# ScalarE writes the masks of units 33 to 46 into the score banks, in place of eight TensorE products per unit

## The chip, the cores and the metric

One core of one Trainium2 chip runs the whole program. The time is device microseconds (us) of one launch. Engines: PE is TensorE (PEld its weight loads, which overlap its matmuls), DVE is VectorE, ACT is ScalarE, POOL is GpSimd, SP is SyncE, which only issues transfers here.

## The reference

Three attention layers over 32 sequences of 64 tokens, 128 features, 16 heads of 64. Layer 0 is causal self-attention, layer 1 attends to a context and is followed by a feed-forward block, layer 2 attends to the same context with rotary embeddings. Each layer ends with a residual and a layer norm. The part that the change touches is layer 2:

```python
q = rope((x @ Wq).reshape(B, Sq, H, Dh)).transpose(0, 2, 1, 3) / sqrt(Dh)
k = rope((ctx @ Wk).reshape(B, Skv, H, Dh)).transpose(0, 2, 1, 3)
scores = jnp.einsum('bhqd,bhkd->bhqk', q, k)
scores = jnp.where(mask[:, None, None, :], scores, -1e9)
attn = jax.nn.softmax(scores, axis=-1)
out = jnp.einsum('bhqk,bhkd->bqhd', attn, v).reshape(B, Sq, H * Dh) @ Wo
```

## The kernel before

A unit is two sequences, 128 tokens, one to each half of the partitions. Each layer has 16 units, so there are 48: 0 to 15 are layer 0, 16 to 31 layer 1, 32 to 47 layer 2. The program runs in steps, -2 to 49, one for each unit with two ahead and two behind; every engine has its own list of work for a step, written by hand, and they meet through semaphores only. In step u the kernel computes the scores and the softmax of unit u, projects queries (u even) or keys (u odd) of units ahead, projects values of unit u, and finishes unit u-2 (weighted values, output product, layer norm).

**PSUM.** Four banks, `ps_a`, hold the scores of one unit. In layer 2 each holds 256 columns: four heads of 64 keys. Four other banks, `ps_p`, are a ring. `fills(u)` lists what PE puts into it in step u, in order, and who empties it: A for ACT, D for DVE. A fill waits until the bank of four fills before has been emptied. In a layer 2 step the list is PP0, PP1 (transposed probabilities of unit u-2, A), two projection banks (D), O0, O1 (weighted values of unit u-2, A), two projection banks (D), V0, V1 (values of unit u, A), Y (output product, D). A step whose follower projects queries (u odd, up to 43) adds T at its end, the transposed input that this projection reads; ACT copies it to `xT_hi` and DVE takes the rest, `xT_lo`. Steps 33 and 35 also hold a feed-forward chunk: FT, F1 (two banks, A, line 804) before Y, and F2 (line 734) after it.

**PE, step u of layer 2.** First `scores(u)`: wait until the exponentials of unit u-1 have been read out of the banks (`exped`), then eight small matmuls that put the mask of unit u into the four banks (line 561: a broadcast mask row times `fold`, two stacked 32x32 identities; `start=True`), then wait for the rotated keys, then 128 small matmuls that add the scores on top (line 571). PE uses 32x64 tiles of its array for both. Then the ring in the order above. PP1 (line 678) waits for `normed_rest`, the second half of the normalised probabilities, and the first projection bank after a T waits for `xT_hi` and `xT_lo`.

**DVE.** Row maxima (line 1029), two turned projection banks (line 956), two more, one half of the normalisation of unit u-1 (line 1074), sums of unit u (line 1059), reciprocal, then Y and its statistics, then `xT_lo` where there is a T (line 943). DVE runs in this order, so `xT_lo` stands ahead of the next unit's maxima.

**ACT.** The empties that `fills` gives it, and between them the exponentials, 8 instructions of 64 columns each half: PP0 and PP1 (line 793), exponentials 0 (line 827), O0 and O1 (line 781), exponentials 1, V0 and V1 (line 791), F1 if there is one, then `normalise_rest(u - 1)` (line 851, 8 instructions, which raise `normed_rest`), then T (line 784) if there is one.

**Masks in layers 0 and 1.** For units 1 to 30 (`masked_by_scalar`), ACT writes the mask into the banks ahead (`put_masks`, line 845), and PE's scores add onto it. Units 0, 31 and all of layer 2 have PE write it.

Of the kernel before, what the change touches and what calls it, by code (L numbers as in the profile page):

```python
# [7 lines left out]
ACT = mybir.ActivationFunctionType  # L8
# [5 lines left out]
B, S, E = 32, 64, 128  # L14
H, D = 16, 64
PAIRS = H // 2
UNITS = B // 2
# [3 lines left out]
N = LAYERS * UNITS  # L21
# [37 lines left out]
def split_heads(u):  # L59

    return 2 * UNITS <= u < N
# [32 lines left out]

def masked_by_scalar(u):

    return 0 < u < 2 * UNITS - 1


def turned_by(u):  # L100
# [180 lines left out]
def build(nc, a, out):  # L281
    ctx = ExitStack()
    with ctx:
# [250 lines left out]
        def _(pe):  # L534
# [7 lines left out]
            def scores(u):  # L542
# [6 lines left out]
                if layer == 2:  # L549
                    if u == 2 * UNITS:  # L550
                        pe.wait_ge(setup_dve, FOLD)

                        pe.wait_ge(headed, HEADED.before(u))


                    for i in range(4):
                        for b in range(2):
                            of = slice(32 * i, 32 * i + 32)
                            own = (i // 2) ^ b
                            m = mask[of, 1, u % UNITS, own:own + 1, :]  # L560
                            mm(ps_a[64 * b:64 * b + 64, i ^ b, 0:256], fold[of, :], m.broadcast_to([32, 4, S]),
                               start=True, stop=False, skip_group_check=True)

                    pe.wait_ge(rotated, ROTATED.at(u - 1 - v, "Kr", 3, v))
                    for quad in range(H // 4):
                        for half in range(2):
                            for i in range(4):
                                for b in range(2):
                                    t = (2 * v + b) * S
                                    of = slice(32 * i, 32 * i + 32)  # L570
                                    last = mm(ps_a[64 * b:64 * b + 64, i ^ b, 64 * quad:64 * quad + 64],  # L571
                                              qT[of, par, 2 * quad + half, t:t + S], kT[of, par, 2 * quad + half, t:t + S],
                                              start=False, stop=half == 1, skip_group_check=True)
                    last.then_inc(scored, 1)
                    return
# [175 lines left out]
            for u in range(FIRST, END):  # L751
                if u in (0, READY):
                    pe.wait_ge(setup_dve, MASKED if u else FIRST_MASKED)

                late = u % 2 == 0 and masked_by_scalar(u)
                if attends(u) and u != N - 1 and not late:
                    scores(u)
                if u - 1 in BIAS_STEPS:
# [17 lines left out]
        def _(act):  # L776
# [61 lines left out]

            def put_masks(u):

                act.wait_ge(setup_dve, FIRST_MASKED if u < READY else MASKED)
                m = mask[:, u // UNITS, u % UNITS, 0:1, :].broadcast_to([128, PAIRS, S])
                for j in range(2):
                    act.wait_ge(shifted, SHIFTED.at(u - 1, j))
                    nc.scalar.activation(ps_a[:, j, :].rearrange("q (p k) -> q p k", k=S), m, ACT.Copy).then_inc(masked, 1)  # L845
# [30 lines left out]
            for u in range(FIRST, END):  # L876
# [4 lines left out]
                if by_head(u):  # L881
# [4 lines left out]
                    for at, (name, j, who) in enumerate(fills(u)):  # L886
                        if "A" not in who:
                            continue
                        while waiting and ((name, j) == ("V", 0) or (name, j) == ("O", 0) and len(waiting) == 2):
                            exponentials(u, waiting.pop(0))  # L890
                        empty(u, at, name, j)
                        if (name, j) == (("F1", 1) if ffn_chunk(u) is not None else ("V", 1)):
                            split_high(u, after_input=True)
                            if by_head(u - 1):
                                normalise_rest(u - 1)
# [485 lines left out]
```

## Time and profile before

| | us |
|---|---|
| Median of 3 runs | 514.36 |
| Lowest and highest | 513.75 to 515.39 |
| The profiled execution, its own time | 513.52 |
| Span of that execution in the trace | 511.6 |
| PE busy | 495.3 (97%) |
| PE's weight loads busy | 462.6 (90%) |
| DVE busy | 426.8 (83%) |
| ACT busy | 394.2 (77%) |
| POOL busy | 315.0 (62%) |

The profiled execution took 1.9 us more than its span, and 0.84 us less than the median. Busy shares are averages over three layers; layer 2 runs from about 334 to 511 us of the span. A row of the timeline merges neighbouring instructions of one line: its length runs from the first start to the last end. Since an engine starts the next instruction before the recorded end of the one before, the time that an instruction really takes of its engine is read from start to start.

### The profile page before, as it was taken

The page shows a single profiled execution, that of the slowest core. Times are in us where ns is not written, and L with a number is a line of the kernel's source. Part 1 is how long each engine was busy: PE and PEld are TensorE (multiplying, and loading weights), DVE is VectorE, ACT ScalarE, POOL GpSimd, SP SyncE. Part 2 cuts the span into 40 slices and gives each one's busy share as a digit, 9 for nine tenths or more (in the row PEclk, how much of TensorE's full clock was granted, in tenths as well). Part 3 has the DMA queues.
Part 4 walks back from the last instruction along what each step waited for, and adds up shares of the span by engine and source line. Part 5 has one row for each costly group of instructions (what it writes and reads, how often), then busy time and mean ns, then how long its engine had stood idle before and what let it go on. Part 6 is the DMA issues. An engine that isn't in the chain of part 4 may idle for free.

```text
span 511.6 us, 23583 instructions
## 1 busy us (share of the span) xinstructions
PE 495.3 (97%) x10188; PEld 462.6 (90%) x10188; DVE 426.8 (83%) x757; ACT 394.2 (77%) x1048; POOL 315.0 (62%) x611
## 2 busy tenths in 40 slices
PE   8989999999999999999999999899999999999995
PEld 7879989989999999999999997789999999999985
DVE  5998988977899788777878779898989888889883
ACT  6877868868988788767878685778778887888761
POOL 3617567546448554454645338878777887788735
PEclk9999999999999999999999999999999999999999
DMA  8910000000021010000000000000000000000000
GB/s 244 361 64 14 3 13 13 9 8 13 3 83 46 5 42 3 2 4 2 3 3 3 3 3 3 2 4 3 4 6 10 15 8 9 8 14 8 9 8 24
DMA packets 10199, 13.79 MB, mean 27 GB/s; under 512 B 880, under 2 KB 7408, under 8 KB 10096
## 3 DMA queue, kind: packets, MB, share of 16 engines
q1 hardware_dynamic: 10096, 12.28, 7.6%
q8 instruction: 81, 1.33, 1.1%
q14 instruction: 22, 0.18, 0.1%
HBM read 11.23 MB, written 1.05 MB: 24 GB/s over the span
## 4 chain that ended last, share of the span: by engine, by line
PE 83%; DVE 6%; ACT 6%; POOL 3%; issue 2%; POOLq 0%; DVEq 0%; ACTq 0%
PE ps_p L712 15%; PE ps_p L538 9%; PE ps_p L539 8%; PE ps_p L540 8%; PE ps_p L678 7%; PE ps_a L597 6%; PE ps_a L619 6%; PE ps_a L571 4%; PE ps_p L667 4%; PE ps_p L669 4%; PE ps_p L668 4%; PE ps_p L619 3%; PE ps_p L734 2%; DVE turn L956 2%; ACT ps_a L845 1%
## 5 line engine op out<-in xcount | busy, mean ns | idle before, releaser
L712 PE MATMUL ps_p<-wo,headsT 128*128 128x128 f32 x768 | 94.0, 275 | 1.4 <-DVE headsT L964 0.9
L712 PEld LDWEIGHTS ps_p<-wo,headsT 128*128 128x128 f32 x768 | 90.4, 192 | 3.0 <-ACT headsT L781 1.0
L1248 POOL TENSOR_TENSOR small<-mv,epsilon 128x1 f32<-128x1 f32 x48 | 10.5, 218 | 133.2 <-DVE mv L985 133.2
L956 DVE TENSOR_TENSOR turn<-ps_p,rope 128x1024 f32<-128x1024 f32 x64 | 76.1, 1222 | 10.9 <-PE ps_p L540 9.3
L791 ACT ACTIVATE vv<-ps_p 128x512 f32<-128x512 f32 x96 | 56.2, 617 | 14.0 <-PE ps_p L669 12.2
L811 ACT ACTIVATE headsT<-ps_a 128x512 f32<-128x512 f32 x60 | 32.6, 596 | 39.5 <-PE ps_a L619 39.5
L827 ACT ACTIVATE probs<-ps_a,top 128x64 f32<-128x64 f32 x256 | 56.0, 354 | 5.8 <-DVE top L1029 3.1
L538 PE MATMUL ps_p<-xT_hi,wq_hi 128*128 128x256 f32 x192 | 59.0, 307 | 0.5 <-DVE xT_lo L943 0.3
L1059 DVE TENSOR_REDUCE total<-probs 128x16 f32<-128x1024 f32 x48 | 58.1, 1211 | 0.4 <-ACT probs L837 0.2
L1033 DVE TENSOR_REDUCE top<-ps_a 128x8 f32<-128x512 f32 x64 | 41.1, 684 | 20.7 <-PE ps_a L597 20.7
L799 ACT ACTIVATE qT<-ps_p,columns 128x256 f32<-128x256 f32 x126 | 49.0, 477 | 8.1 <-PE ps_p L540 8.1
L539 PE MATMUL ps_p<-xT_lo,wq_hi 128*128 128x256 f32 x192 | 54.5, 284 | 0.0
L540 PE MATMUL ps_p<-xT_hi,wq_lo 128*128 128x256 f32 x192 | 54.4, 283 | 0.0
L678 PE MATMUL ps_p<-eye,probs 128*128 128x128 f32 x384 | 51.1, 275 | 1.5 <-ACT vv L791 0.8
L678 PEld LDWEIGHTS ps_p<-eye,probs 128*128 128x128 f32 x384 | 43.4, 141 | 7.6 <-ACT vv L791 0.9
L1208 POOL TENSOR_TENSOR qT<-turn 128x512 f32<-128x512 f32 x32 | 43.6, 1386 | 8.4 <-DVE turn L956 8.4
L1208 POOL TENSOR_TENSOR kT<-turn 128x512 f32<-128x512 f32 (+1 forms) x40 | 44.9, 1148 | 5.2 <-DVE turn L956 5.2
L799 ACT ACTIVATE kT<-ps_p,columns 128x256 f32<-128x256 f32 x124 | 47.1, 497 | 0.7 <-PE ps_p L540 0.6
L1074 DVE TENSOR_TENSOR probs<-probs,rinv 128x512 f32<-128x512 f32 x62 | 44.2, 751 | 1.0
L962 DVE COPY probsT<-ps_p 128x512 f32<-128x512 f32 x58 | 37.2, 683 | 3.3 <-PE ps_p L678 3.3
L538 PE MATMUL ps_p<-cT_hi,wk_hi 128*128 128x256 f32 x128 | 39.0, 304 | 0.6
L538 PEld LDWEIGHTS ps_p<-xT_hi,wq_hi 128*128 128x128 f32 x192 | 37.3, 194 | 1.4 <-issue 0.4
(149 smaller groups left out, 1400.0 us busy)
## 6 DMA issues: line engine op xcount, KB each, us to landing
out<-y_out SPq DMA_DIRECT2D x16, 64.0 KB, 2.6
raw<-in_x_turned SPq DMA_DIRECT2D x1, 768.0 KB, 9.2
across<-in_across SPq DMA_DIRECT2D x1, 704.0 KB, 7.3
raw<-in_ctx_turned SPq DMA_DIRECT2D x5, 128.0 KB, 2.6
wq_raw<-in_L_xattn_sa_wq SPq DMA_DIRECT2D x2, 256.0 KB, 2.9
wk_raw<-in_L_xattn_sa_wk SPq DMA_DIRECT2D x2, 256.0 KB, 4.2
wv_raw<-in_L_xattn_sa_wv SPq DMA_DIRECT2D x1, 512.0 KB, 5.6
wo<-in_L_xattn_sa_wo SPq DMA_DIRECT2D x1, 512.0 KB, 6.7
```

The costliest lines, as they stand in the source:

```text
L538: mm(dst, w[0], x[0], start=True, stop=False)
L539: mm(dst, w[0], x[1], start=False, stop=False)
L540: return mm(dst, w[1], x[0], start=False, stop=True)
L619: before, last = last, mm(head_bank(u, b)[64 * c:64 * c + 64, 64 * p:64 * p + 64], vv[of, w % 2, c, p, :], probsT[of, p // HALF, q:q + 64] ...
L678: last = nc.tensor.transpose(bank[:, 128 * pp:128 * pp + 128], probs[:, unit % 2, at_head:at_head + 2, :].rearrange("q h k -> q (h k)"), e ...
L712: last = mm(bank[:, 0:E], headsT[:, p, :, :].rearrange("r b q -> r (b q)"), wo[:, layer % 2, p, :], start=(p == 0), stop=(p == PAIRS - 1))
L791: ins = nc.scalar.activation(vv[:, u % 2, j, :, :].rearrange("k p d -> k (p d)"), bank[:, :], ACT.Copy)
L799: ins = nc.scalar.activation(to[:, g % 2, p, :], bank[:, CT * k:CT * k + CT], ACT.Identity, bias=bias[:, g * CU // UNITS, p:p + 1])
L827: ins = nc.scalar.activation(probs[:, u % 2, n, :], ps_a[:, bank, 64 * k:64 * k + 64], ACT.Exp, bias=top[:, at:at + 1], scale=scale)
L956: ins = V.tensor_tensor(turn[:, j % 2, :, :].rearrange("d a (h b t) -> d a h b t", h=2, t=S), bank[:, None, :].broadcast_to([128, 2, 512]) ...
L1059: V.tensor_reduce(total[:, :], probs[:, u % 2, :, :], AX_X, ALU.add).then_inc(dve_step, 1)
L1208: G.tensor_tensor(to[:, projected(u) % 2, 2 * j:2 * j + 2, of], *[t[:, :, of] for t in turned(j)], ALU.add).then_inc(rotated, 1)
```

## The change

The masks of units 33 to 46 are written by ACT too. `put_masks(u)` gets a form for layer 2: it waits for the second half of the exponentials of unit u-1, which ACT itself has just issued, and writes the mask with two instructions, each over two banks of 256 columns. It stands directly behind the exponentials of the unit ahead, so ahead of V0 and V1. PE's eight mask matmuls of those 14 units go, and `scores` waits for `masked` in their place. Units 32 and 47 keep the matmuls. The condition `late`, which in layers 0 and 1 puts the scores of even units behind the weighted values, is held to those layers, so the place of the scores in layer 2 stays.

```diff
@@ def masked_by_scalar(u):
-    return 0 < u < 2 * UNITS - 1
+    return 0 < u < 2 * UNITS - 1 or 2 * UNITS < u < N - 1
@@ scores(u), layer == 2
-                    for i in range(4):
-                        for b in range(2):
-                            of = slice(32 * i, 32 * i + 32)
-                            own = (i // 2) ^ b
-                            m = mask[of, 1, u % UNITS, own:own + 1, :]
-                            mm(ps_a[64 * b:64 * b + 64, i ^ b, 0:256], fold[of, :], m.broadcast_to([32, 4, S]),
-                               start=True, stop=False, skip_group_check=True)
+                    if masked_by_scalar(u):
+                        pe.wait_ge(masked, MASKED_BANK.at(u - 1, 1))
+                    else:
+                        for i in range(4):
+                            for b in range(2):
+                                of = slice(32 * i, 32 * i + 32)
+                                own = (i // 2) ^ b
+                                m = mask[of, 1, u % UNITS, own:own + 1, :]
+                                mm(ps_a[64 * b:64 * b + 64, i ^ b, 0:256], fold[of, :], m.broadcast_to([32, 4, S]),
+                                   start=True, stop=False, skip_group_check=True)
@@ PE's loop over the steps
-                late = u % 2 == 0 and masked_by_scalar(u)
+                late = u % 2 == 0 and masked_by_scalar(u) and u < 2 * UNITS
@@ put_masks(u)
+                if split_heads(u):
+                    act.wait_ge(exped, EXPED.at(u - 1, 1))
+                    m = mask[:, 1, u % UNITS, 0:1, :]
+                    for j in range(2):
+                        nc.scalar.activation(ps_a[:, 2 * j:2 * j + 2, 0:256].rearrange("q m (f k) -> q m f k", k=S),
+                                             m[:, None, :, :].broadcast_to([128, 2, 4, S]), ACT.Copy).then_inc(masked, 1)
+                    return
@@ ACT's loop over fills(u), by_head(u)
                         while waiting and ((name, j) == ("V", 0) or (name, j) == ("O", 0) and len(waiting) == 2):
                             exponentials(u, waiting.pop(0))
+                            if not waiting and masked_by_scalar(u + 1):
+                                put_masks(u + 1)
```

ACT's order in step 37, a step of layer 2 that ends with a T, and into the next. Before (`ps_a` is read by the exponentials):

```order
L781 ACTIVATE headsT<-ps_p 128x8x64 [waits filled] x2
L827 ACTIVATE probs<-ps_a,top 128x64 [waits dve_step]
L827 ACTIVATE probs<-ps_a,top 128x64 x7
L791 ACTIVATE vv<-ps_p 128x512 [waits filled] x2
L851 ACTIVATE probs<-probs,inv 128x64 [waits dve_step]
L851 ACTIVATE probs<-probs,inv 128x64 x7
L784 ACTIVATE xT_hi<-ps_p 128x2x128 [waits filled]
```

After, the same place (the changed file's line numbers are 3 to 10 higher: 784 for 781, 830 for 827, 794 for 791, 861 for 851, 787 for 784):

```order
L784 ACTIVATE headsT<-ps_p 128x8x64 [waits filled] x2
L830 ACTIVATE probs<-ps_a,top 128x64 [waits dve_step]
L830 ACTIVATE probs<-ps_a,top 128x64 x7
L848 ACTIVATE ps_a<-mask 128x2x256 [waits exped]
L848 ACTIVATE ps_a<-mask 128x2x256
L794 ACTIVATE vv<-ps_p 128x512 [waits filled] x2
L861 ACTIVATE probs<-probs,inv 128x64 [waits dve_step]
L861 ACTIVATE probs<-probs,inv 128x64 x7
L787 ACTIVATE xT_hi<-ps_p 128x2x128 [waits filled]
```

Two instructions have come in, the first with a wait for ACT's own exponentials; V0 and V1, the normalisation and T all stand behind them. On PE, where step 38 ends and step 39 begins, before:

```order
L712 MATMUL ps_p<-wo,headsT 128x128 [waits act_emptied,dve_emptied]
L712 MATMUL ps_p<-wo,headsT 128x128 x7
L561 MATMUL ps_a<-mask,fold 64x256 [waits exped]
L561 MATMUL ps_a<-mask,fold 64x256 x7
L571 MATMUL ps_a<-kT,qT 64x64 [waits rotated]
L571 MATMUL ps_a<-kT,qT 64x64 x63
L678 MATMUL ps_p<-eye,probs 128x128 [waits normed,dve_emptied]
```

After (715 for 712, 574 for 571, 681 for 678):

```order
L715 MATMUL ps_p<-wo,headsT 128x128 [waits act_emptied,dve_emptied]
L715 MATMUL ps_p<-wo,headsT 128x128 x7
L574 MATMUL ps_a<-kT,qT 64x64 [waits rotated,masked,exped]
L574 MATMUL ps_a<-kT,qT 64x64 x63
L681 MATMUL ps_p<-eye,probs 128x128 [waits normed,dve_emptied]
```

The eight mask matmuls are gone, and their wait has moved to the first score matmul, with `masked` beside it. DVE, POOL and SP have the same rows in the same order as before.

## Rows read from the trace of the kernel before

**Rows 1.** The page: busy time of each engine, PE's granted clock in 40 slices.

```profile
PE 495.3 (97%) x10188; PEld 462.6 (90%) x10188; DVE 426.8 (83%) x757; ACT 394.2 (77%) x1048; POOL 315.0 (62%) x611
...
PEclk9999999999999999999999999999999999999999
```

**Rows 2.** Waits of PE's weight loads, 334 to 492 us: total us, times, longest.

```profile
PEld ps_a L561 <- issue: 1.3, 8, 0.2
PEld ps_p L678 <- ACT vv L791: 0.9, 1, 0.9
PEld ps_p L538 <- DVE turn L956: 0.6, 2, 0.3
```

**Rows 3.** Timeline of PEld and PE, step 38: start us, length us, engine, line.

```profile
402.26 0.12 PEld L561 LDWEIGHTS ps_a<-mask,fold 32*64 32x64 bf16 x8 [0.17 <-issue]
402.26 0.32 PE L561 MATMUL ps_a<-mask,fold 32*64 32x256 bf16 x8
402.29 1.51 PEld L571 LDWEIGHTS ps_a<-kT,qT 32*64 32x64 f32 x128
402.39 1.54 PE L571 MATMUL ps_a<-kT,qT 32*64 32x64 f32 x128
...
404.69 0.20 PEld L538 LDWEIGHTS ps_p<-xT_hi,wq_hi 128*128 128x128 f32 x1
```

**Rows 4.** Timeline of ACT, step 37 into step 38.

```profile
398.26 1.75 ACT L827 ACTIVATE probs<-ps_a,top 128x64 f32<-128x64 f32 x8
399.84 1.15 ACT L791 ACTIVATE vv<-ps_p 128x512 f32<-128x512 f32 x2
400.86 2.02 ACT L851 ACTIVATE probs<-probs,inv 128x64 f32<-128x64 f32 x8
402.77 0.38 ACT L784 ACTIVATE xT_hi<-ps_p 128x256 fp32r<-128x256 f32 x1
404.56 1.09 ACT L793 ACTIVATE probsT<-ps_p 128x512 f32<-128x512 f32 x2 [1.41 <-PE ps_p L678]
405.53 1.76 ACT L827 ACTIVATE probs<-ps_a,top 128x64 f32<-128x64 f32 x8
407.54 1.09 ACT L781 ACTIVATE headsT<-ps_p 128x512 f32<-128x512 f32 x2 [0.26 <-PE ps_p L619]
```

**Rows 5.** Timeline of ACT, steps 38 and 39, and PEld's transposes of step 39.

```profile
410.09 1.15 ACT L791 ACTIVATE vv<-ps_p 128x512 f32<-128x512 f32 x2
411.11 2.01 ACT L851 ACTIVATE probs<-probs,inv 128x64 f32<-128x64 f32 x8
...
420.13 1.15 ACT L791 ACTIVATE vv<-ps_p 128x512 f32<-128x512 f32 x2
...
413.90 0.86 PEld L678 LDWEIGHTS ps_p<-eye,probs 128*128 128x128 f32 x8
```

**Rows 6.** Timeline of ACT in layer 1: a pair of masks, and what follows.

```profile
201.25 1.11 ACT L845 ACTIVATE ps_a<-mask 128x512 f32<-128x512 bf16 x2
202.29 2.29 ACT L799 ACTIVATE qT<-ps_p,columns 128x256 f32<-128x256 f32 x6
```

**Rows 7.** Timeline of DVE, step 37 into step 38.

```profile
403.43 0.39 DVE L943 TENSOR_TENSOR xT_lo<-ps_p,xT_hi 128x256 fp32r<-128x256 f32 x1
403.97 1.22 DVE L1029 TENSOR_REDUCE top<-ps_a 128x16 f32<-128x1024 f32 x1 [0.15 <-PE ps_a L571]
405.79 2.36 DVE L956 TENSOR_TENSOR turn<-ps_p,rope 128x1024 f32<-128x1024 f32 x2 [0.59 <-PE ps_p L540]
```

**Rows 8.** Timeline of ACT and DVE across a T of the feed-forward step 35.

```profile
382.07 0.38 ACT L784 ACTIVATE xT_hi<-ps_p 128x256 fp32r<-128x256 f32 x1 [1.03 <-PE ps_p L657]
...
382.49 0.43 DVE L943 TENSOR_TENSOR xT_lo<-ps_p,xT_hi 128x256 fp32r<-128x256 f32 x1 [0.21 <-ACT xT_hi L784]
```

**Rows 9.** Timeline of ACT and PEld, feed-forward step 33.

```profile
350.59 1.76 ACT L827 ACTIVATE probs<-ps_a,top 128x64 f32<-128x64 f32 x8
352.17 1.22 ACT L791 ACTIVATE vv<-ps_p 128x512 f32<-128x512 f32 x2
353.49 1.57 ACT L804 ACTIVATE hT<-ps_p,columns 128x256 f32<-128x256 f32 x4
...
355.67 1.87 PEld L734 LDWEIGHTS ps_p<-w,hT 128*128 128x128 f32 x16
```

**Rows 10.** Timeline of ACT and PEld, feed-forward step 35.

```profile
374.51 1.76 ACT L827 ACTIVATE probs<-ps_a,top 128x64 f32<-128x64 f32 x8
...
379.76 1.87 PEld L734 LDWEIGHTS ps_p<-w,hT 128*128 128x128 f32 x16
```

## The prediction

> **What bounds the kernel now.** I read the page first: PE is busy 97% of the span, ACT 77%, and PE's granted clock stands in the top tenth in all 40 slices [rows 1], so PE runs at its upper level (2.4 GHz) throughout. Then the waits of PE in layer 2: between 334 and 492 us PE's loads waited for another engine some 1.5 us in all [rows 2]. So layer 2 is bound by PE's own list of work: steps take 10.25 and 10.04 us in turn, as the starts of V0 show (399.84, 410.09, 420.13), 20.29 for two [rows 4, 5].
>
> A bound PE does not mean that the others have room. The question is how much later ACT may finish before PE has to wait for it, so I read ACT's timeline over one step. ACT waits twice: 1.41 us ahead of PP and 0.26 us ahead of O [rows 4]. Everything between V0 and the next PP stands behind the new instructions, and two things of it are waited for by PE. One is `normed_rest` (the end of line 851), the other is `xT_hi` (line 784), through DVE's `xT_lo`.
>
> **What the change takes from PE.** In step 38 the loads of the mask matmuls start at 402.26 and those of the scores at 402.29; the matmuls start at 402.26 and 402.39 [rows 3]. Eight of them cost PE 0.03 us by the loads and 0.13 us by the matmuls, since they run side by side on different tiles. I take 0.13, as the matmuls' starts set when the scores end. 14 units: 1.8 us, at least 0.4. The gap of 0.17 ahead of them [rows 3] stays: the score matmuls use the same tiles.
>
> The Trainium skill, "TensorE: Matmul & The Clock Gate", Back-to-back issue gap, gives 262 cycles for an isolated matmul of 256 columns, 0.109 us. Eight in a row would be 0.87 us, and the change would take 12.2 us off PE, not 1.8. The trace has all eight behind each other's starts in 0.13 us, so it is the packing that the same page describes, and the row decides.
>
> **What it adds to ACT.** The nearest rows are the pairs of masks in layers 0 and 1: the same 512 columns from the same tile into PSUM. One pair starts at 201.25 and the next work at 202.29: 1.04 us [rows 6]. A wait comes with it. ACT starts V0 at 399.84, 0.17 us ahead of the recorded end of the exponentials (398.26 + 1.75 = 400.01) [rows 4]. The first mask waits for that end, and a releaser's end stands 0.04 us ahead of the waiter's start where I can see one (382.07 + 0.38 = 382.45, DVE at 382.49) [rows 8]. So ACT loses 0.17 + 0.04 = 0.21, and V0, V1, the normalisation and T come 1.04 + 0.21 = 1.25 us later. Call this A. From below: no overlap lost, A = 1.04. From above: the form over two banks has no row, and its two instructions might overlap nothing. One mask alone lasts 1.11 less half of 1.04, 0.59; two are 1.18, and with 0.21 A is about 1.40. I take 1.25, nearest to the rows of masks.
>
> The scores themselves do not wait for the masks. Both are written by 400.05 + 1.1 = 401.2, and PE comes to the scores at 402.26. V0's bank is wanted by a fill of the next step's PP, V0 drained at about 401.7: hidden too. If A passed 2.2 us both covers would be gone.
>
> **Where A meets PE: `normed_rest`.** In step 38 line 851 ends at 411.11 + 2.01 = 413.12. PE's loads for PP0 and PP1 start at 413.90, eight in 0.86, so the fifth, which needs it, starts about 413.90 + 4 x 0.10 = 414.31 [rows 5]. Room: 1.19, less 0.04 for the signal, 1.15. A exceeds it by 0.10, so PP1 comes 0.10 us later than before, and PE's 0.13 are lost to waiting. What follows carries this on: PP1, two projection banks, O, then ACT's O, exponentials 1, masks, V, normalisation. That is a ring through both engines, so the delay repeats in each step of this kind and cannot be caught up.
>
> **Where A meets PE: T.** In step 37 T starts at 402.77, pushed only by the normalisation ahead of it [rows 4]. Later by A: 404.02, ends 404.40. DVE takes `xT_lo` at 404.44, for 0.39, to 404.83 (before: 403.43) [rows 7]. PE's first load of the query projection stood at 404.69 [rows 3]; with 0.06 for the signal it starts at 404.89: 0.20 later than before, 0.33 later than it could. DVE's maxima stand behind `xT_lo`: 1.22 us to about 406.0 where they ended at 405.19, and DVE's next row started at 405.79, held by PE [rows 7]; it moves by about 0.2. Exponentials 0 move from 405.53 to 406.05 and end by start-to-start time (1.58) at 407.6, O's turn was 407.54 and is now 407.74 [rows 4]: hidden. So a step behind a T costs 0.20.
>
> **The sum.** Steps 38, 40, 42 and 44: 4 x 0.20 = 0.8. `normed_rest` in steps 37, 39, 41, 43, 45 and 46: 6 x 0.10 = 0.6. Step 33, the first with the masks ahead: 0.1.
>
> The feed-forward steps have another meeting. F2 (line 734) waits for the last F1 that ACT empties, and these stand behind V. Step 33: exponentials end 352.35, masks 352.39 to 353.43, V 1.02, F1 1.57: 356.02, plus 0.04 is 356.06 where the loads stood at 355.67 [rows 9]: 0.4. Step 35: exponentials end 376.27, then 0.04 + 1.04 + 1.02 + 1.57 + 0.04 is 379.98 where the loads stood at 379.76 [rows 10]: 0.2. Step 35's `normed_rest` adds 0.1; in step 36 PE keeps about 0.1 of its saving, as T had 1.03 us of idle ahead of it [rows 8]. Together 0.6.
>
> Sum: 0.8 + 0.6 + 0.1 + 0.6 = 2.1 us longer. PE's 1.8 us do not come off this: at every place PE waits, and its saving turns into idle time. On the profiled execution: span 511.6 + 2.1 = 513.7, its own time 513.52 + 2.1 = 515.6; on the median, 514.36 + 2.1 = 516.5.
>
> Each 0.1 us of A counts at some 14 places: 1.4 us. A = 1.04 gives 2.1 - 2.9 = 0.8 shorter, 513.5 on the median; A = 1.40 gives 2.1 + 2.1 = 4.2 longer, 518.6.
>
> **Rivals.**
>
> 1. *ACT's idle time covers it* (faster). Where A is below about 0.9 (1.15 less the 0.13 by which PE comes sooner at `normed_rest`, 1.25 less 0.33 at T), nothing of it reaches PE, and all of 1.8 us comes off: 512.6. For: ACT is busy 77% [rows 1], and its wait ahead of PP alone is 1.41 [rows 4]. Against: a pair of masks alone takes 1.04 [rows 6]. Chance 0.12.
>
> 2. *The wait costs less than the recorded end says*: A about 1.14, as if only the 0.10 or so by which wide instructions overlap were lost. Then each place costs 0.1 less, 2.1 - 1.5 = 0.6 longer: 515.0. The Trainium skill, "ScalarE: Activation LUTs", What ACT_TABLE_LOAD costs, puts the overlap of ACT's neighbours at 93 ns, less than the 0.17 of the row; with it A would be 1.17 and the sum about 1.0 us. No run here shows such a wait on ACT. Chance 0.22.
>
> 3. *The form costs more*: the two-bank write or the wait for its own result is dearer, A about 1.5: 2.1 + 3.5 = 5.6 longer, 520. For: neither the form nor a wait of ACT on itself has a row. Against: columns set the length of ACT's other rows. Chance 0.14.
>
> The Trainium skill, "TensorEngine Tiling (Array Packing)", PSUM Bottleneck, warns that tiling speeds up TensorE but not the emptying of PSUM, which can become the bound. The rows fit it: the change moves 0.13 us of packed work to an engine where it takes 1.04.
>
> **How the numbers follow.** The forecast, A near 1.25, has 0.52, and its own range is 515.4 to 517.8. A measurement of this kernel can tell about 0.3%, 1.5 us, from no change: under 512.8 is faster, over 515.9 slower. Faster is rival 1: 0.12. Slower is rival 3 and most of the forecast (0.14 + 0.42 = 0.56). The rest is 0.32. The range runs from A = 1.04 to a little over A = 1.40, 513.3 to 518.9, and leaves out rival 1 and the upper end of rival 3.
>
> **What would show it.** Right: two rows of masks behind each exponentials 1 of about 1.1 us; V0 about 1.25 later behind the exponentials; ACT's wait ahead of PP down from 1.41 to 0.2 or less; new waits of PE on ACT (line 851) and on DVE's `xT_lo`, each 0.2 to 0.35; two steps taking 20.6 us where they took 20.29. Wrong: no such waits, and two steps of 20.03 (rival 1); a gap behind the exponentials other than 0.04, or mask rows well away from 1.1 (rivals 2 and 3). It would also be wrong if the maxima behind the later `xT_lo` held DVE, and with it PE's third projection bank, by more than the 0.2 above.

## The result: 5.6 us slower, and where the time went

| | before | after |
|---|---|---|
| Median, us | 514.06 (6 runs) | 519.69 (6 runs) |
| Lowest and highest, us | 513.38 to 515.39 | 518.24 to 522.62 |
| Ratio | | 1.0109, 95% interval 1.0085 to 1.0133 |
| The profiled execution, its own time and span, us | 513.52, 511.6 | 522.62, 520.8 |

Slower, as forecast, but 5.6 us where 2.1 were forecast, and above the range. The profiled execution of the changed kernel is the longest of its six; its stretches are read with that in mind.

The page of the changed kernel answers [rows 1]: ACT has 16.8 us more work, DVE what it had, PE's loads 1.5 us more. PE's busy time has grown by 4.8 us, though 112 matmuls went, and one slice of its granted clock is no longer in the top tenth.

```profile
PE 500.1 (96%) x10076; PEld 464.1 (89%) x10076; DVE 426.6 (82%) x757; ACT 411.0 (79%) x1076; POOL 315.5 (61%) x611
...
PEclk9999999999999999999999999999999899999999
...
q8 instruction: 80, 1.31, 1.1%
```

ACT's timeline from step 37 into step 38 answers [rows 4] (start us, length us, engine, line, operation, in square brackets the idle time ahead):

```profile
399.61 1.76 ACT L830 ACTIVATE probs<-ps_a,top 128x64 f32<-128x64 f32 x8
401.39 1.12 ACT L848 ACTIVATE ps_a<-mask 128x512 f32<-128x512 bf16 x2
402.45 1.06 ACT L794 ACTIVATE vv<-ps_p 128x512 f32<-128x512 f32 x2
403.41 2.01 ACT L861 ACTIVATE probs<-probs,inv 128x64 f32<-128x64 f32 x8
405.32 0.37 ACT L787 ACTIVATE xT_hi<-ps_p 128x256 fp32r<-128x256 f32 x1
407.92 0.60 ACT L796 ACTIVATE probsT<-ps_p 128x512 f32<-128x512 f32 x1 [2.23 <-PE ps_p L681]
```

The masks stand 401.39 - (399.61 + 1.76) = 0.02 behind the recorded end of the exponentials and take 402.45 - 401.39 = 1.06 of ACT. V0 started 1.58 behind the exponentials' start before (399.84 - 398.26), and 2.84 now: 1.26 later, where A was put at 1.25. ACT does what was forecast. But then it waits 2.23 us for PP, where it should have waited next to nothing. PE's loads say why; their waits, 334 to 502 us (total us, times, longest), answer [rows 2]:

```profile
PEld ps_a L574 <- issue: 4.7, 10, 1.8
PEld ps_p L681 <- issue: 2.9, 7, 1.5
PEld ps_p L681 <- ACT vv L794: 0.9, 1, 0.9
PEld ps_p L622 <- issue: 0.8, 2, 0.4
PEld ps_p L538 <- DVE xT_lo L955: 0.6, 2, 0.3
```

The new time has the releaser "issue", time in which the profile shows nothing that is waited for. That label alone proves nothing: a wait that stands in a semaphore instruction of its own, as the one for `normed_rest`, gets it too. PE's timeline of steps 38 to 40 settles it for the long ones: each stands in the middle of a run of equal instructions, the scores in two cases, the transposes in the third, at one that waits for nothing:

```profile
403.60 1.52 PE L574 MATMUL ps_a<-kT,qT 32*64 32x64 f32 x120
406.81 0.34 PE L574 MATMUL ps_a<-kT,qT 32*64 32x64 f32 x8 [1.69 <-issue]
...
419.67 0.27 PE L574 MATMUL ps_a<-kT,qT 32*64 32x64 f32 x2 [1.09 <-issue]
...
431.71 0.87 PE L681 MATMUL ps_p<-eye,probs 128*128 128x128 f32 x6 [1.23 <-issue]
```

After the first of them PE runs slowly for a while. Windows of the changed kernel (busy time of each engine, then PE's granted clock):

```profile
404.00:407.40 3.40, 1.71 (x112) 1.50 (x99) 1.40 (x6) 1.69 (x7) 2.17 (x7) 1.00 0.02 5
407.50:410.90 3.40, 3.40 (x19) 3.40 (x17) 1.72 (x2) 2.72 (x10) 0.42 (x1) 0.50 0.09 24
411.00:414.00 3.00, 3.00 (x80) 2.79 (x79) 2.21 (x3) 1.70 (x7) 2.53 (x2) 1.00 0.00 0
```

PE was busy 1.71 of 3.40 us, and then for 3.4 us the granted clock is 0.50, the lower level (1.2 GHz): always busy, with 19 matmuls. What it costs can be read from starts: from the first transpose to the first weighted value PE took 411.10 - 407.09 = 4.01 us, and 406.33 - 403.87 = 2.46 before, so 1.55 more. That is a part of the 4.8 us by which PE's busy time grew. The rest is not traced to a place here: a later execution without such a stretch (e11) still has 498.0 us, against 495.3 before.

**A measure of the stage.** From the start of the first instruction behind the scores of step 32 to that behind the scores of step 46 is the part with 14 changed units. I call it the stage. Before: 335.6 to 484.7, 149.1 us. After: 335.6 to 493.4, 157.8 us, 8.7 longer. The pauses with nothing awaited, of over 0.2 us each, add up to 6.3 of it (0.48, 0.54 and the five of the table below) and the stretch at half clock to 1.55, 7.8 in all. That leaves 0.9 for the ring, not the 2.1 that were forecast. The two overlap: while PE pauses, ACT catches up. The loads' waits fit that, with two waits for `xT_lo` here where four were forecast.

### The profile page after: what moved, and what is told of

Its sections match the earlier page's. It is cut to its first block, busy times and chain, and to the rows that moved or that the text cites. A ratio compares the mean times of both kernels' runs of the same rounds, so it can differ in the third digit from the quotient of the medians.

```text
span 520.8 us, 23401 instructions
## 1 busy us (share of the span) xinstructions
PE 500.1 (96%) x10076; PEld 464.1 (89%) x10076; DVE 426.6 (82%) x757; ACT 411.0 (79%) x1076; POOL 315.5 (61%) x611
## 3 DMA queue, kind: packets, MB, share of 16 engines
q8 instruction: 80, 1.31, 1.1%
HBM read 11.23 MB, written 1.05 MB: 24 GB/s over the span
## 4 chain that ended last, share of the span: by engine, by line
PE 79%; ACT 8%; DVE 6%; issue 3%; POOL 2%; DMA 1%; POOLq 0%; SPq 0%; DVEq 0%; ACTq 0%
PE ps_p L715 15%; PE ps_p L538 9%; PE ps_p L539 7%; PE ps_p L540 7%; PE ps_p L681 7%; PE ps_a L600 6%; PE ps_a L622 6%; PE ps_a L574 4%; PE ps_p L670 4%; PE ps_p L622 4%; PE ps_p L672 3%; PE ps_p L671 3%; PE ps_p L737 2%; ACT ps_a L855 1%; ACT headsT L814 1%
## 5 line engine op out<-in xcount | busy, mean ns | idle before, releaser
L794 ACT ACTIVATE vv<-ps_p 128x512 f32<-128x512 f32 x96 | 54.8, 598 | 13.5 <-PE ps_p L672 11.6
L538 PE MATMUL ps_p<-xT_hi,wq_hi 128*128 128x256 f32 x192 | 59.7, 311 | 0.7 <-DVE xT_lo L955 0.3
L681 PE MATMUL ps_p<-eye,probs 128*128 128x128 f32 x384 | 53.2, 278 | 3.0 <-issue 1.2
L538 PEld LDWEIGHTS ps_p<-xT_hi,wq_hi 128*128 128x128 f32 x192 | 38.0, 198 | 2.3 <-issue 0.9
L538 PE MATMUL ps_p<-cT_hi,wk_hi 128*128 128x256 f32 x128 | 39.0, 305 | 0.7
```

What stands on the lines that cost most here:

```text
L538: mm(dst, w[0], x[0], start=True, stop=False)
L681: last = nc.tensor.transpose(bank[:, 128 * pp:128 * pp + 128], probs[:, unit % 2, at_head:at_head + 2, :].rearrange("q h k -> q (h k)"), e ...
L794: ins = nc.scalar.activation(vv[:, u % 2, j, :, :].rearrange("k p d -> k (p d)"), bank[:, :], ACT.Copy)
```

## What the pauses have in common

I numbered PE's instructions in the traces (weight loads, matmuls, and those of its semaphore instructions that the trace holds) in order of their start. Each pause of over 0.2 us behind 100 us in which PE waits for no semaphore lies ahead of an instruction whose number is 193 above a multiple of 256: in the changed kernel 14529, 15553, 16065, 16577 and 17089 among them, and in the kernel before 3777 and 11969, its only two. The same holds for all experiments. The page names a queue of instructions, q8: 80 packets with 1.31 MB, so 16 KB each, for some 20,600 instructions of PE: one packet for 256 instructions. So PE's program arrives in blocks of 256, and PE pauses where a block begins.

The transfers' records then give each block three numbers. "Run" is the time that PE took for the 256 instructions ahead of the block, without the pause. The pause is counted from start to start; the brackets of the timelines hold the idle time alone and are 0.2 to 0.3 us shorter. "Start" is the start of the block's packet against the moment PE entered the block ahead. "Lead" is from the packet's start to the block's first instruction:

| kernel, step, block's first instruction | run | start | lead | pause |
|---|---|---|---|---|
| before, steps 37 to 46, shorter block of each | 3.89 to 3.98 | +0.70 to +1.26 | 2.67 to 3.21 | 0 |
| after, 38, 15553 | 2.29 | +1.87 | 2.32 | 1.90 |
| after, 39, 16065 | 1.67 | +0.56 | 2.42 | 1.31 |
| after, 40, 16577 | 1.67 | +0.97 | 2.20 | 1.50 |
| after, 41, 17089 | 2.36 | +0.28 | 2.39 | 0.31 |
| after, 42, 17601 | 2.90 | +0.82 | 2.29 | 0.21 |
| after, 43, 18113 | 3.32 | +0.09 | 3.23 | 0.00 |
| before, 35, 14017 | 1.95 | -0.79 | 2.75 | 0.00 |

The four columns are tied: start + lead = run + pause (1.87 + 2.32 = 2.29 + 1.90). The fetch mostly begins once PE has entered the block ahead, so only one block ahead, and no lead is under 2.2 us, in any of the traces. A block that PE runs through in 1.7 us is too short for that. The scores are such a burst: 256 instructions in about 1.5 us. Before, in steps 37 to 46, a boundary fell inside each burst, far from its ends, so that PE had slower work on both sides of it in each block (3.9 us and more). The two blocks of before's layer 2 that ran under 2 us (1.80 in step 34, 1.95 in step 35) had a fetch that started 0.8 us early. The change takes 16 instructions out of each unit and puts in one wait that the trace counts: 15 fewer per unit, so the boundary moves through the burst, and in steps 38 to 40 a block covers the burst whole.

The Trainium skill, "Runtime: NRT & Kernel Launch", Instruction fetch mechanics, says that instructions are "refilled in 16 KiB blocks (256 instructions)", and that the cost of crossing a boundary is "one DMA tail-bump, mostly hidden", because engines issue more slowly than blocks arrive. The size agrees (81 packets of 16 KB before). The second does not hold here: small tiles let PE take 256 instructions in 1.67 us, and the lead is 2.2 us or more. The Trainium skill gives PE room there for 2048 instructions, eight blocks, and says too that the sequencer fetches the next page while it executes the current one; the packets' starts show the latter, a fetch one block ahead.

## The experiments

Two theories from here on. **F** (fetch): the time beyond the ring's 2.1 us comes from the place of block boundaries in PE's bursts. **R** (ring, or a loss per changed unit): it comes from the longer waits between ACT, DVE and PE, and the pauses only show where PE idles. Earlier expectations word them in their own way. Each kernel was timed beside the kernel before on its chip (medians 514.2 to 514.6); "stage" is as above, 149.1 us before.

**e1. Both engines write the masks.** PE's mask matmuls come back, behind the wait for ACT's. They overwrite ACT's masks with the same values.

```diff
@@ scores(u), layer == 2, of the changed kernel
                     if masked_by_scalar(u):
                         pe.wait_ge(masked, MASKED_BANK.at(u - 1, 1))
-                    else:
-                        for i in range(4):
+                    for i in range(4):
...
```

> The changed kernel with PE's eight mask matmuls of units 33 to 46 put back behind the new wait: both engines write the same masks. This is the whole ACT part of the change, with PE's list of instructions as long as before (but for one wait per unit). Theory R (the ring through ACT alone explains the loss, A costs more than worked out): all of the loss stays or grows a little, 519 to 521 us, since PE does more. Theory F (PE's stream stalls for 1 to 2 us where the removal of 16 instructions per unit moved a place 512 instructions apart into the burst of scores; the ring costs only what was worked out): no pause inside the scores with nothing awaited, and 1.5 to 3.5 us over the kernel before, about 516 to 517.5 us.

Measured: 518.25 us (518.07 to 518.92), ratio 1.0079 (1.0059 to 1.0099), between the two expectations. Stage 152.7, begun 1.0 later than before's, with one pause of 1.46 (step 35). PE's timeline:

```profile
369.82 1.25 PE L573 MATMUL ps_a<-kT,qT 32*64 32x64 f32 x94
372.32 0.37 PE L573 MATMUL ps_a<-kT,qT 32*64 32x64 f32 x14 [1.24 <-issue]
```

Without that pause the stage is about 151.2, 2.1 above before: what ACT's masks cost by themselves. PE's matmuls on top cost nothing (e7 below, without them, has the same 151.2), so their removal gains nothing: PE waits for ACT there. Both points are the ones the prediction made of the ring; most of the rest of after's loss is missing here. The pause is ahead of number 14017, the table's last row, where before had none: run 2.11 and start +0.92 here, 1.95 and -0.79 there.

**e6. No masks in units 33 to 46**, from either engine (the values of layer 2 differ). ACT's order is then that of before; PE alone is changed.

```diff
@@ scores(u), layer == 2, of the changed kernel
-                    if masked_by_scalar(u):
-                        pe.wait_ge(masked, MASKED_BANK.at(u - 1, 1))
-                    else:
+                    if not masked_by_scalar(u):
...
-                                              start=False, stop=half == 1, skip_group_check=True)
+                                              start=half == 0 and masked_by_scalar(u), stop=half == 1,
+                                              skip_group_check=True)
@@ ACT's loop
-                            if not waiting and masked_by_scalar(u + 1):
+                            if not waiting and masked_by_scalar(u + 1) and u < 2 * UNITS - 1:
```

> PE's part alone: the mask matmuls of units 33 to 46 are left out and ACT writes none (the masks of these units are left out of the computation). PE's instructions are as many as in the changed kernel less one wait for each unit; ACT's list is as before. Theory R: 1.8 us faster than before, 512.5 us. Theory F in its simple form (the place in the stream decides alone): up to 1.8 us less, plus pauses of 3 to 5 us, so 514 to 518 us. Theory F with timing (a pause needs the place near the end of the scores and also that PE comes to the preceding place with nothing ahead of it): between the two.

Measured: 518.12 us (515.88 to 520.22), ratio 1.0078 (1.0049 to 1.0106). **Less work on PE, nothing added anywhere, and slower.** The profiled execution (516.42, one of the shorter) has a stage of 151.2, with this pause in it in step 40, at number 16577, where after has one too:

```profile
426.58 0.88 PE L680 MATMUL ps_p<-eye,probs 128*128 128x128 f32 x6 [1.79 <-issue]
```

This speaks hardest against R, which expected 512.5: there is no ring's delay here at all. With e8's stage below the sum closes: 148.1 and the three pauses of over 0.4 us (2.06, 0.44, 0.48) are 151.1.

**e8. The same without masks, and 128 instructions more at the program's start** (64 matmuls of one column, whose results nothing reads), which shifts all later boundaries by half a block. **e7** is the changed kernel with that pad.

```diff
+            def pad(rounds):
+                for _ in range(rounds):
+                    for i in range(4):
+                        for b in range(2):
+                            of = slice(32 * i, 32 * i + 32)
+                            mm(ps_a[64 * b:64 * b + 64, i ^ b, 0:1], eye_bf[of, 0:64], eye_bf[of, 0:1],
+                               start=True, stop=True, skip_group_check=True)
@@ ahead of PE's loop over the steps
+            pad(8)
```

> As the kernel with PE's part alone (the masks of units 33 to 46 left out on both engines), with 128 more PE instructions at the program's start. Theory F: no pauses in steps 36 to 46, and what PE's masks cost shows: 1.8 us less than before plus up to 1 us of the pad, 512.6 to 513.6 us.

Measured: 515.93 us (514.2 to 517.75), ratio 1.002 (0.9999 to 1.004), against 1.0078 without the pad: 2.2 us less with 128 instructions more, but not the 512.6 to 513.6 expected. In the traced execution (514.54, one of the shorter) the stage is 148.1, without a pause: 1.0 shorter than before, 0.07 us per unit. That is what PE's masks cost PE; the prediction took 0.13. Two things outside the stage eat that up. A block in step 47 is now too short, as PE's timeline shows below. And the stage starts at 336.1 instead of 335.6. That this is the pad's price is not shown: e1 and e9, without a pad there, start at 336.6 and 336.4. All of e1, e7, e8 and e9 ran at half clock near 29 us (granted 0.50 from 28.9 to 32.1 in e1 and e8, 1.00 before), but so did e6, which starts at 335.8.

```profile
493.13 1.83 PE L723 MATMUL ps_p<-wo,headsT 128*128 128x128 f32 x15 [1.34 <-issue]
```

> The changed kernel with 64 tiny matmuls (128 PE instructions) once, at the program's start, where PE waits for the first input. Theory F: no pauses of over 1 us in steps 36 to 46, no burst of the pad in front of layer 2, and what is left is the ring: 2 to 3.5 us over the kernel before, 516.5 to 518 us. Theory R: no change from the changed kernel, 519.7 us.

Measured: 519.25 us (517.31 to 520.29), ratio 1.0101 (1.0061 to 1.014). The profiled execution is the one of 517.31: stage 151.2, which is 149.1 + 2.1, and no pause in it. Among its loads' waits (334 to 490) are the two that the prediction named, for `xT_lo` (L538) and, under "issue", for `normed_rest` (L690):

```profile
PEld ps_p L690 <- issue: 2.4, 8, 0.6
PEld ps_a L583 <- issue: 1.2, 7, 0.2
PEld ps_p L538 <- DVE turn L978: 1.1, 4, 0.4
PEld ps_p L538 <- DVE xT_lo L965: 1.1, 4, 0.3
```

Its span is 515.4 = 511.6 + 0.7 (ahead of the stage) + 2.1 + 1.0 (the block in step 47). Its median however lies hardly lower than after's (ratio 1.0101 against 1.0109), and near the 519.7 that R expected, not at F's 516.5 to 518. The three other executions are 2 to 3 us longer, and they were not traced. So e7 shows the mechanism in one execution and does not show a gain in the median.

**e2 and e5. Pads of 128 and 64 instructions ahead of the scores of step 32** in the changed kernel, e3 (400) and e4 (128) the same in the kernel before. The pad is that of e7 with `fold[of, :]` in place of `eye_bf[of, 0:64]`.

```diff
@@ scores(32), of the changed kernel (e2: 8, e5: 4) and of the kernel before (e3: 25, e4: 8)
+                        pad(8)
```

> The changed kernel with 64 tiny mask-shaped matmuls (128 PE instructions, about 1.1 us) once, ahead of the scores of unit 32. Nothing else moves. Theory R: the loss plus 1.1 us, about 520.5 us, pauses as they were or anywhere. Theory F: the places of the stall move 128 instructions away from the end of the scores in all steps of layer 2, the pauses of 1.7, 1.1 and 1.2 us go, and the time falls below that of the changed kernel, to about 516.5 to 518 us in spite of the pad.

Measured: 519.94 us, ratio 1.0109 (1.0092 to 1.0125), nearer to R's 520.5 than to F's 518. No pause in steps 36 to 46, which take 102.7 us (108.7 after, 101.3 before). But the pad is a burst itself, and 128 instructions of it with the scores made a short block (run 1.38), with a pause in these scores and then 3.4 us at half clock; another pause of 1.55 came in step 47:

```profile
333.98 1.09 PE L584 MATMUL ps_a<-kT,qT 32*64 32x64 f32 x82
336.87 0.76 PE L584 MATMUL ps_a<-kT,qT 32*64 32x64 f32 x46 [1.81 <-issue]
```

The median settles nothing then; the place of the pauses counts.

> The changed kernel with 32 tiny matmuls (64 PE instructions, about 0.5 us) once, ahead of the scores of unit 32. In the changed kernel the stalls stood at every 512th instruction of PE (the 193rd), where that place fell 16 ahead of the end of the scores to 4 behind it (steps 38 to 40), and drifted by 8 to 12 a step. Theory F: with 64 more instructions the same places reach the end of the scores in steps 44 to 46; the pauses of over 1 us leave steps 38 to 40 and show in 44 to 46 if anywhere. Theory R or chance: pauses stay in steps 38 to 40, or are spread.

Measured: 525.08 us (524.7 to 525.33), ratio 1.0207 (1.0174 to 1.024). Half the shift puts the boundary's passage through the burst's end into later steps, and the pauses went there, to steps 44 and 46. Two more stand in the scores of step 32 behind the pad (2.23) and behind those of step 33 (1.61); steps 38 to 40 have none:

```profile
469.49 1.51 PE L584 MATMUL ps_a<-kT,qT 32*64 32x64 f32 x118
473.05 0.35 PE L584 MATMUL ps_a<-kT,qT 32*64 32x64 f32 x10 [2.05 <-issue]
...
496.78 0.81 PE L691 MATMUL ps_p<-eye,probs 128*128 128x128 f32 x6 [1.37 <-issue]
```

32 matmuls of one column (64 instructions) move the pauses from some steps to others. That R can't give.

> The kernel before with 200 tiny mask-shaped matmuls (400 PE instructions, about 3.3 us) once, ahead of the scores of unit 32; ACT as before. Theory R: 3.3 us over the kernel before, 517.5 us, with no pause inside the scores. Theory F: the places 512 apart fall within 35 instructions of the end of the scores in steps 36 to 46, where they stood about 100 to 145 ahead of it, so pauses of about 1 to 1.7 us come in several of these steps: 3.3 plus 5 to 15 us, 522 to 533 us.

Measured: 522.71 us, ratio 1.0158 (1.0139 to 1.0178). Two pauses at the pad (2.29 inside it, 1.76 in the scores behind it), which alone bring the median into F's range. Behind them next to none (0.38 and 0.23), although from step 36 on blocks covered the burst whole. **In its strong form, a block over a burst always pauses, F fell here.** The packets' records show what saved them: run 1.35 to 2.2, but the packets mostly started 0.4 to 1.3 us *ahead* of PE's entry into the block before (-0.40 to -1.32, at either end -0.08 and +0.09), lead 2.3 to 2.7.

> The kernel before with 64 tiny matmuls (128 PE instructions, about 1.1 us) once, ahead of the scores of unit 32. Theory R: 1.1 us over the kernel before, 515.3 us. Theory F with places 512 apart: the same, 515.3 us, since the places then stand 220 to 270 instructions ahead of the scores' end, which is at or before their start. Theory F with places 256 apart: they fall at the scores' end in steps 40 to 46, and the time is 5 us or more over that.

Measured: 520.23 us (518.3 to 520.46), ratio 1.0105 (1.0082 to 1.0129). 2.01 in the scores behind the pad, and in the steps after it pauses of 0.54 at 400.1, 0.96 at 410.8, 0.54 at 431.1 and 0.59 at 451.4, each at a boundary, now the other one of the two in a step. Step 38's stands ahead of a large matmul of the projection that waits for nothing:

```profile
410.83 0.39 PE L540 MATMUL ps_p<-xT_hi,wq_lo 128*128 128x256 f32 x1 [0.68 <-issue]
```

With runs of 2.5 to 2.8 and starts of +0.86 to +0.96 it paused, with 1.35 to 1.42 and starts of -1.10 to -1.54 (steps 43 to 46) it did not. A start of -0.55 was not early enough for a run of 1.56: that is the 0.59 at 451.4. So a pause needs both, a short block and a fetch that is not early enough for it. All 13 traces together say the same: of 70 blocks with a run under 2.3 us, 18 had a fetch that started 0.3 us or more behind PE's entry into the block before, and all 18 have a pause of 1.1 to 2.3 us; of the other 52 none has one of over 0.6.

**e9. The pad spread out.** The changed kernel; behind the wait for `masked`, each of units 33 to 36 has 16 mask matmuls of one column. They add the mask once more to one column of each bank, so the values differ. 128 instructions in all, no burst of their own.

```diff
@@ scores(u), layer == 2, of the changed kernel, behind the masks
+                        for i in range(4 * (2 if u < 2 * UNITS + 5 else 0)):
+                            for b in range(2):
+                                of = slice(32 * (i % 4), 32 * (i % 4) + 32)
+                                own = (i % 4 // 2) ^ b
+                                m = mask[of, 1, u % UNITS, own, 0:1]
+                                mm(ps_a[64 * b:64 * b + 64, (i % 4) ^ b, 0:1], fold[of, :], m,
+                                   start=False, stop=True, skip_group_check=True)
```

> The changed kernel with 128 instructions more on TensorE, in small portions: behind its masked scores, each of units 33 to 36 also gets 16 mask matmuls of one column (32 instructions), ahead of the transposes of the probabilities. They add the mask once more to one column of each bank, so the values differ. Theory F (TensorE's instructions come in blocks of 256, and a block that lies wholly inside a burst of scores comes too late): the burst now passes the block's boundary 128 instructions away from where it did, so no pause with nothing awaited in steps 36 to 46, scores of step 32 to scores of step 46 in 151 to 152.5 us (157.8 in the changed kernel), median 516.0 to 517.5. Rival R (the time lost lies in the waits of the ring ScalarE, VectorE, TensorE that the change made longer, the pauses only show where TensorE idles): 128 more instructions on TensorE, which waits in every step, change nothing: pauses of 1 us and more stay in steps 38 to 40, 157 to 159 us, median 519.5 to 521.

**e10. The change for units 39 to 46 only.** PE writes units 33 to 38 as before; the boundary's drift starts later and does not reach the end of the burst.

```diff
-    return 0 < u < 2 * UNITS - 1 or 2 * UNITS < u < N - 1
+    return 0 < u < 2 * UNITS - 1 or 2 * UNITS + 6 < u < N - 1
```

> The change for units 39 to 46 only; units 33 to 38 have TensorE's masks, as before. Theory F: the position of the scores' bursts against the blocks of 256 instructions starts to drift seven units later, and does not come to the places where a block lies wholly inside a burst; no pause of over 0.5 us; only the ring's price, for 8 units of 14: 2.1 times 8/14 = 1.2 us; median 515.2 to 516.0. Rival R (a loss per changed unit, of whatever cause, 5.3 us over 14 units): 8/14 of it, 3.0 us, median 517.0 to 517.6.

**e11. The changed kernel itself**, beside these two.

> The changed kernel itself, beside the two others on the same chip. Theory F: the pauses stand at the same instructions, one each in steps 38, 39 and 40, 1.0 to 1.8 us each, whichever execution is profiled, or are missing together where a fetch happened to start early enough; scores of step 32 to step 46 in 155 to 158.5 us; median 518.5 to 520.5. Rival R: the time as steady as before's, pauses at other instructions or none, with the same length of the stage.

Measured, all three in turn on one chip, before at 514.21 (17 runs):

| | median, us | ratio, 95% interval | stage, us | pauses of over 0.35 us in the stage |
|---|---|---|---|---|
| e11 | 519.61 (517.41 to 522.83) | 1.0107 (1.0071 to 1.0143) | 155.4 | 0.46, 0.54, 1.38, 2.05, 0.59 |
| e9 | 517.83 (516.18 to 518.70) | 1.0069 (1.0045 to 1.0093) | 151.4 | 0.41 |
| e10 | 515.26 (514.13 to 516.19) | 1.0022 (1.0008 to 1.0037) | 150.4 | none |

e10 is F's case: 8 of 14 units, 1.05 us slower in the median (0.4 to 1.9), stage 1.3 longer, where the ring's share is 2.1 x 8/14 = 1.2. R's 3.0 lies outside. e9 has lost the pauses of steps 38 to 41 with 128 instructions *more*, and its stage is 2.3 above before. Its median is 1.8 lower than e11's, with ranges that overlap, and 0.3 above what F expected: it has a pause of 1.55 in step 47, which I had not reckoned with, as e2 and e8 have. Its loads' waits show the ring's two meetings, one in each step. The second row has the releaser "issue", but it is the wait for `normed_rest`: the semaphore's instruction stands ahead of it, and ACT's normalisation ended at 414.24 + 2.01 = 416.25:

```profile
414.24 2.01 ACT L868 ACTIVATE probs<-probs,inv 128x64 f32<-128x64 f32 x8
...
406.63 0.19 PEld L538 LDWEIGHTS ps_p<-xT_hi,wq_hi 128*128 128x128 f32 x1 [0.27 <-DVE xT_lo L962]
416.37 0.42 PEld L688 LDWEIGHTS ps_p<-eye,probs 128*128 128x128 f32 x4 [0.19 <-issue]
```

e11 repeats the pauses of steps 39 and 40 at the same numbers (16065, 16577), but step 38 passes without one. PE's timeline there:

```profile
403.27 1.59 PE L574 MATMUL ps_a<-kT,qT 32*64 32x64 f32 x128
404.80 1.09 PE L681 MATMUL ps_p<-eye,probs 128*128 128x128 f32 x8
```

The program is the same, the run of the block too (2.24 against 2.29); the packet started 0.75 us ahead of PE's entry into the block before, where after's started 1.87 behind it. No pause, and no stretch at half clock behind it. F had allowed "one each in steps 38, 39 and 40, or missing together"; that was wrong in the second half: each boundary is a draw of its own. This one, 1.9 us and the 1.55 that half clock cost, is worth 3.4 us. That it makes the spread of after's executions (518.24 to 522.62) is not shown: before's spread by as much (512.89 to 516.34 beside e5 to e8).

## Why the prediction was wrong: right ring, missing term

**A, the delay on ACT.** Forecast 1.25 (1.04 + 0.17 + 0.04). Measured 1.26: 1.06 from mask to V, and 0.02 between the exponentials' end and the mask, so 1.06 + 0.17 + 0.02, with rounding. Rivals 2 and 3 stood on this and both fall: the two-bank form costs what two single masks do, and ACT's wait for its own result costs the overlap of 0.17. The Trainium skill's 93 ns for that overlap, "ScalarE: Activation LUTs", was named under rival 2; the trace has 0.17 + 0.02.

**Rival 1**, the delay hidden: falls with the same rows.

**What PE's masks cost.** Forecast 0.13 a unit; e8's one trace shows 1.0 / 14 = 0.07. So even covered the change could have given 1.0 us, not 1.8. Mis-sized, without effect on the sum, since the saving was to be lost in waits. e1 shows that it is.

**`normed_rest`.** Forecast 0.10 later than before; with the true saving of 0.07 that is a wait of 0.17. e9's row has 0.19. ACT's wait ahead of PP, forecast 0.2 or less, is 0.20 there (ACT at 416.45). **T through `xT_lo`.** Forecast 0.20 later, so a wait of 0.27; e9's row has 0.27. **The feed-forward steps.** F2 of step 33 stood at 355.67 [rows 9] and starts at 356.13 after: 0.46, forecast 0.4 and the 0.1 of step 33. F2 of step 35: 379.76 [rows 10] to 380.53, 0.77 in all, forecast 0.7:

```profile
356.13 1.86 PEld L737 LDWEIGHTS ps_p<-w,hT 128*128 128x128 f32 x16
...
380.53 1.86 PEld L737 LDWEIGHTS ps_p<-w,hT 128*128 128x128 f32 x16
```

**Two steps.** Forecast 20.6 where they took 20.29. In the changed kernel, where no pause lies between, ACT's V0 shows 480.71 - 460.10 = 20.61:

```profile
460.10 1.06 ACT L794 ACTIVATE vv<-ps_p 128x512 f32<-128x512 f32 x2
470.24 1.07 ACT L794 ACTIVATE vv<-ps_p 128x512 f32<-128x512 f32 x2
480.71 1.06 ACT L794 ACTIVATE vv<-ps_p 128x512 f32<-128x512 f32 x2
```

**The sum of the ring.** Forecast 2.1. Stages without pauses: 151.2 - 149.1 = 2.1 (e7), 2.1 (e1 less its pause), 2.3 (e9, with 0.4 of a pause), and for 8 units 1.3 where 1.2 follows.

**The step that failed** is the first one: "layer 2 is bound by PE's own list of work". I costed removed matmuls by their time on PE and never asked what a shorter list does to its supply. The sum has no term for it. In the two traces of the changed kernel it is 8.7 - 2.1 = 6.6 and 6.3 - 2.1 = 4.2 us of the stage; in the median of its runs 5.6 - 2.1 = 3.5. The pauses themselves are larger, since they hide a part of the ring's waits. The experiments show the term in the traced stages; for the median e6, e8, e9 and e10 bear it out and e7 does not. The trace of before did show it, small: one pause of this kind outside layer 2, at number 3777, and the chip's fetches stood on the page as q8:

```profile
105.31 0.34 PE L597 MATMUL ps_a<-kT,qT 64*64 64x64 f32 x7 [0.60 <-issue]
```

No row of layer 2 said how near its blocks came to a pause. My range of 513.3 to 518.9 was made from A alone, and A was right to 0.01.

**What stays open.** What sets the start of a fetch, from 1.5 us ahead of PE's entry into the block before to 2.0 behind it in the short blocks, and up to 3.6 in long ones of steps 37 to 41 of after: PE enters the block, the packet mostly starts 0.5 to 1.3 us later, but in e3 and in the last steps of e4 it came earlier, steadily, and in after and e11 the same boundary had both. I found no rule, and no experiment varied it alone. Open too are e7's three longer executions, and e2 to e5 can't be read by their medians, as the pads bring pauses of their own.

## What to carry to other kernels

Where TensorE issues hundreds of small-tile instructions in a burst, count them in blocks of 256: a block that it runs through in less than about 3.5 us (some 1 us to the fetch's start, 2.2 to 2.8 to its use) may pause for up to 2 us with nothing awaited. This is what these 13 traces show, not a limit measured by itself. An edit that changes the number of instructions shifts every later boundary, so a kernel with less work can be slower (e6), and one with 128 more instructions faster (e8 against e6); compare variants by a stage without such pauses, and look for rows with "issue" in the middle of a group before explaining a difference by waits. The delay of an engine that stands in a ring with the bound one can be added up from start times to 0.1 us, as here; it pays to ask of the bound engine what feeds it.

## What the hardware showed that I had not expected

- PE's instructions come in packets of 16 KB for 256 instructions, one block ahead; from a packet's start to the block's first instruction it took never less than 2.2 us, and in pauses up to 2.8.
- The pauses are 1.1 to 2.3 us in all 18 blocks of the 13 traces with a run under 2.3 us and a fetch that started 0.3 us or more behind PE's entry into the block ahead, and under 0.6 in the 52 with an earlier fetch; they differ between executions of the same kernel (1.90 and 0.01 at the same instruction).
- A pause can be followed by 3.4 us at a granted clock of 0.50, with PE busy throughout. Of the pauses of 1.90, 1.31 and 1.50 us in after only the first was, and e11's of 2.05 was not, so not each one is.
- Eight mask matmuls of 256 columns, side by side on tiles of 32x64, cost TensorE 0.07 us in all (e8's stage against before's, one trace of each), less than the 0.13 between their first and the next group's start [rows 3].
- ACT's wait for its own result costs it 0.02 behind the recorded end, and the overlap of 0.17 that it has otherwise.
